# A six-layer decoder kernel on one core: ternary values fetched two banks at a time, and three small moves between engines

## The reference

```python
x = _layernorm(x + attention_int4(x))         # 32 heads, inputs and weights quantised
x = _layernorm(x + cross_attention(x, ctx))
x = _layernorm(x + expert_feedforward(x))
x = _layernorm(x + attention(x))              # 64 heads
x = _layernorm(x + long_convolution(ctx, ctx, x))
x = _layernorm(x + ternary_feedforward(x))
```

```python
def bitlinear158(x, w, b):                    # w is ternary after weight_quant
    return act_quant(rms_norm(x)) @ weight_quant(w).T + b
h = gelu(silu(bitlinear158(x, w1, b1)))       # 512 -> 2048
h = layer_norm(h, ln_g, ln_b)
x = _layernorm(x + bitlinear158(h, w2, b2))   # 2048 -> 512
```

## Time and profile before

| | us |
|---|---|
| median of three runs | 1980.08 |
| lowest, highest | 1978.74, 1982.89 |
| profiled execution, its own time | 1984.86 |
| its span, first to last instruction | 1983.1 |

### The profile page before, as it was taken

How to read it: one execution, slowest core, us unless ns; L and a number is a source line. 1 busy time by engine, 2 the same in 40 slices (tenths; PEclk the granted TensorE clock), 3 DMA queues, 4 the chain that set the end, 5 groups by cost and what they waited for, 6 DMA issues and landing times. The chain is left out here.

```text
span 1983.1 us, 32214 instructions
## 1 busy us (share of the span) xinstructions
PE 1737.2 (88%) x11756; PEld 1345.4 (68%) x11774; DVE 1398.1 (71%) x2871; ACT 1034.5 (52%) x1936; POOL 571.6 (29%) x563
## 2 busy tenths in 40 slices
PE   4489999777868999999999997999998799967876
PEld 2255665423558999999999996888886577734443
DVE  8478888587955666665665665465665699849997
ACT  3436666623414444444444444565565254469994
POOL 6133332144110001000000002223333497944321
PEclk9669999956988999999999998999998899979998
DMA  6498898051611222212222232323225265100001
GB/s 169 42 98 98 93 98 92 28 182 28 209 58 56 57 67 67 78 57 78 65 70 78 62 115 94 112 97 128 75 86 149 81 174 133 45 0 11 22 22 32
DMA packets 148480, 163.87 MB, mean 83 GB/s; under 512 B 46240, under 2 KB 100384, under 8 KB 146528
## 3 DMA queue, kind: packets, MB, share of 16 engines
q1 hardware_dynamic: 143076, 151.85, 33.8%
q10 hardware_dynamic: 5248, 9.96, 1.4%
HBM read 116.86 MB, written 19.48 MB: 69 GB/s over the span
## 5 line engine op out<-in xcount | busy, mean ns | idle before, releaser
L1661 ACT ACTIVATE f_gate<-f_gu 128x256 f32<-128x256 f32 x264 | 98.8, 383 | 270.0 <-PE f_gu L1525 190.3
L1802 DVE TENSOR_TENSOR f_hid<-f_gate,f_gu 128x256 f32<-128x256 f32 x264 | 108.2, 420 | 157.4 <-ACT f_gate L1661 153.6
L570 DVE TENSOR_REDUCE a_rowmax<-a_ring 128x2 f32<-128x512 f32 x256 | 164.9, 687 | 51.3 <-PE a_ring L652 48.9
L2826 PE MATMUL g_p<-e_kv,e_toep 128*128 128x288 f32 x640 | 164.9, 415 | 6.0 <-DVE e_planes L2885 4.2
L523 ACT ACTIVATE a_prob<-a_sT 128x1024 f32<-128x1024 f32 x128 | 130.6, 1026 | 47.7 <-PE a_sT L641 47.7
L2826 PEld LDWEIGHTS g_p<-e_kv,e_toep 128*128 128x128 f32 x640 | 122.2, 195 | 38.7 <-issue 6.6
L1538 PE MATMUL f_gu<-f_lowh,f_bg 128*128 128x256 f32 x704 | 141.5, 283 | 5.2 <-POOL f_lowl L1443 5.0
L1525 PE MATMUL f_gu<-f_xhi,f_wg 128*128 128x256 f32 x704 | 131.3, 284 | 0.0
L1525 PE MATMUL f_gu<-f_xhi,f_wu 128*128 128x256 f32 x704 | 130.4, 283 | 0.0
L1807 DVE TENSOR_TENSOR f_hl<-f_hid,f_hh 128x768 fp32r<-128x768 f32 (+2 forms) x90 | 84.5, 939 | 55.9 <-ACT f_hh L1709 54.8
L1538 PEld LDWEIGHTS f_gu<-f_lowh,f_bg 128*128 128x128 f32 x704 | 115.9, 191 | 9.8 <-POOL f_lowl L1443 5.2
(11 more groups left out here) (436 smaller groups left out, 4848.7 us busy)
## 6 DMA issues: line engine op xcount, KB each, us to landing
f_entry<-in_WdT SPq DMA_DIRECT2D x89, 256.0 KB, 2.8
d_staging<-in_w SPq DMA_DIRECT2D x16, 1024.0 KB, 5.7
a_qs<-a_hi SPq DMA_DIRECT2D x64, 128.0 KB, 7.4
a_ks<-a_hi SPq DMA_DIRECT2D x64, 128.0 KB, 6.1
e_toep<-lags SPq DMA_DIRECT2D x16, 512.0 KB, 3.9
f_entry<-in_Bg SPq DMA_DIRECT2D x89, 64.0 KB, 1.9
f_entry<-in_Bu SPq DMA_DIRECT2D x89, 64.0 KB, 2.0
cf<-in_xT SPq DMA_DIRECT2D x4, 1024.0 KB, 7.8
```

The lines of the kernel that those rows point to most:

```text
L570: dve.tensor_reduce(rowmax[:, s % 2, :, e * SLOTS + j], ring[n % RING][:, :].rearrange("p (q t) -> p q t", t=T), AX.X, ALU.max, negate=Tru ...
L1661: act.activation(gate[:, i % 2, :], gu[n % 3][:, 0, :], ACT.Silu).then_inc(s_["gate_ready"], 1)
L1802: dve.tensor_tensor(hid[:, j, :], gate[:, i % 2, :], gu[n % 3][:, 1, :], ALU.mult).then_inc(s_["hid_ready"], 1)
L2826: last = pe.matmul(py[n % RING][:, 0:YS], toep[:, u, h % 2, (t - j) * P:(t - j + 1) * P], kv[:, h % 2, j, :, :].rearrange("p b c -> p (b c ...
```

## The change

In the attention output, GpSimd keeps the bias of the first three batches (`OTHERS = 3`) and the root steps; VectorE subtracts the bias of the other five and does the residual sum of all tiles, in an instruction that also gives the row's sum, and from it the negative mean. ScalarE takes the sum of squares about the mean. Of the four token loads ahead one stays where it was, and the next stage's SP issues the other three first. In the ternary layer `pq2` is one PSUM tile of two banks, so that the 16 turns of a tile go in two groups of eight and ScalarE fetches 1024 values in one instruction, the first before the squares of s-4 and the second where the four were. GpSimd's add of the bias to tile t waits for L3198 of tile t+2, the one of the same step (for the last tiles, tile 15).

```diff
-                for b in range(3):
+                for b in range(OTHERS):
                     take_bias(b)
-                for i in range(B + 1):
-                    if i < B:
-                        n = i * TB
-                        pool.wait_ge(got_x[i], 16)
-                        pool.wait_ge(s_["y_ready"], n + 1)
-                        pool.tensor_tensor(row_of(rows, n), r[:, n % RR, :], row_of(rows, n), ALU.add
-                                           ).then_inc(s_["sum_even"], 1)
-                    if i + 3 < B:
...
-                            pool.tensor_scalar(stats[:, n, 8:9], stats[:, n, 6:7], stats[:, n, 9:10], -1.0, ALU.mult, ALU.mult
-                                               ).then_inc(s_["root_ready"], 1)
+                for n in range(NT):
+                    pool.wait_ge(s_["square_ready"], n + 1)
+                    pool.tensor_scalar(stats[:, n, 3:4], stats[:, n, 2:3], 1.0 / D, EPS, ALU.mult, ALU.add
+                                       ).then_inc(s_["eps_added"], 1)
+                    pool.wait_ge(s_["eps_added"], n + 1)
+                    pool.tensor_tensor(stats[:, n, 4:5], stats[:, n, 3:4], keep["neghalf"][:, :], ALU.pow
+                                       ).then_inc(s_["root_steps"], 1)
+                    pool.wait_ge(s_["root_steps"], n + 1)
+                    pool.tensor_tensor(stats[:, n, 5:6], stats[:, n, 1:2], stats[:, n, 4:5], ALU.mult
+                                       ).then_inc(s_["root_ready"], 1)
 
...
                 def scale(b):
-                    dve.wait_ge(s_["sub_ready"], b + 1)
+                    if b < OTHERS:
+                        dve.wait_ge(s_["sub_ready"], b + 1)
+                    else:
+                        ch.step(dve.tensor_tensor(flat[:, :, chunks(b), :], flat[:, :, chunks(b), :], wide_of(cbias, b),
+                                                  ALU.subtract))
                     dve.tensor_tensor(flat[:, :, chunks(b), :], flat[:, :, chunks(b), :], wide_of(inv, b), ALU.mult
...
                     for q in range(TB):
                         n = i * TB + q
-                        if 0 <= n < NT:
-                            dve.wait_ge(s_["acc_done"], n + 1)
-                            if n >= RR:
-                                dve.wait_ge(s_["sum_odd" if q else "sum_even"], (n - RR) // TB + 1)
-                            dve.scalar_tensor_tensor(r[:, n % RR, :], acc[n % RING][:, :], unit_tok[:, n:n + 1], wsrow[:, :],
-                                                     ALU.mult, ALU.mult).then_inc(s_["y_ready"], 1)
-                    if i < B:
-                        n = i * TB + 1
-                        dve.wait_ge(got_x[i], 16)
+                        dve.wait_ge(s_["acc_done"], n + 1)
+                        if n >= RR:
+                            dve.wait_ge(s_["summed"], n - RR + 1)
+                        dve.scalar_tensor_tensor(r[:, n % RR, :], acc[n % RING][:, :], unit_tok[:, n:n + 1], wsrow[:, :],
+                                                 ALU.mult, ALU.mult).then_inc(s_["y_ready"], 1)
+                    dve.wait_ge(got_x[i], 16)
+                    for q in range(TB):
+                        n = i * TB + q
                         dve.wait_ge(s_["y_ready"], n + 1)
-                        dve.tensor_tensor(row_of(rows, n), r[:, n % RR, :], row_of(rows, n), ALU.add
-                                          ).then_inc(s_["sum_odd"], 1)
+                        dve.tensor_tensor_reduce(row_of(rows, n), r[:, n % RR, :], row_of(rows, n), 1.0, 0.0, ALU.add, ALU.add,
+                                                 stats[:, n, 0:1]).then_inc(s_["summed"], 1)
+                        dve.wait_ge(s_["summed"], n + 1)
+                        dve.tensor_scalar(stats[:, n, 1:2], stats[:, n, 0:1], -1.0 / D, None, ALU.mult).then_inc(s_["mean_ready"], 1)
                     if i + 2 < B:
                         quantise(i + 2)
-                    for q in range(TB):
-                        n = (i - 1) * TB + q
-                        if 0 <= n < NT:
-                            dve.wait_ge(s_["sum_odd" if q else "sum_even"], n // TB + 1)
-                            tl.step(dve.bn_stats(stats[:, n, 0:6], row_of(rows, n)))
-                            dve.bn_aggr(stats[:, n, 6:8], stats[:, n, 0:6]).then_inc(s_["var_ready"], 1)
 
...
                     for q in range(TB):
+                        n = (i - 1) * TB + q
+                        if 0 <= n < NT:
+                            act.wait_ge(s_["mean_ready"], n + 1)
+                            if n >= TB:
+                                act.wait_ge(s_["square_ready"], n - 1)
+                            act.activation(junk[:, q, :], row_of(rows, n), ACT.Square, bias=stats[:, n, 1:2],
+                                           accum_out=stats[:, n, 2:3]).then_inc(s_["square_ready"], 1)
+                    for q in range(TB):
                         n = (i - 2) * TB + q
                         if 0 <= n < NT:
                             act.wait_ge(s_["root_ready"], n + 1)
-                            act.activation(row_of(rows, n), row_of(rows, n), ACT.Identity, bias=stats[:, n, 8:9],
-                                           scale=stats[:, n, 9:10])
+                            act.activation(row_of(rows, n), row_of(rows, n), ACT.Identity, bias=stats[:, n, 5:6],
+                                           scale=stats[:, n, 4:5])
 
...
                 sp.wait_ge(stored, 16 * B * TB)
-                for n in range(4):
-                    loads.tokens(sp, io, n)
+                loads.tokens(sp, io, 0)
...
+                for n in range(1, 4):
+                    loads.tokens(sp, io, n)
                 sp.dma_start(brow[:, :], io["b1"].broadcast_to([4, INNER])).then_inc(s_["b1_in"], 16)
...
-        pq2 = [mk.ps(f"g_pq2{n}", [P, 512]) for n in range(2)]
+        pq2 = mk.ps("g_pq2", [P, IT // 2 * P])
...
                     t = tile_at(s, 1)
                     if t is not None:
-                        if t >= 1:
-                            pool.wait_ge(s_["q1_ready"], t)
+                        pool.wait_ge(s_["q1_ready"], min(t + 2, NT - 1))
...
+                def second(t, half):
+                    act.wait_ge(s_["q2_turned"], t * 2 + half + 1)
+                    act.activation(q2f[:, t % 2, half * (IT // 2):(half + 1) * (IT // 2), :],
+                                   pq2[:, :].rearrange("p (j t) -> p j t", t=P), ACT.Identity, bias=minus[:, :]
+                                   ).then_inc(s_["q2f_ready"], 1)
 
...
                         act.wait_ge(s_["shifted"], t + 1)
                         act.activation(junk[:, 1, :], hc[:, t % 4, :], ACT.Square, accum_out=row2[:, t, 0:1]).then_inc(s_["ssq2"], 1)
+                    t = tile_at(s, 6)
+                    if t is not None:
+                        if t >= 2:
+                            act.wait_ge(s_["out_done"], t - 1)
...
                     t = tile_at(s, 6)
                     if t is not None:
-                        if t >= 2:
-                            act.wait_ge(s_["out_done"], t - 1)
-                        for n in range(KT):
-                            act.wait_ge(s_["q2_turned"], t * KT + n + 1)
-                            act.activation(q2f[:, t % 2, n * 4:(n + 1) * 4, :], pq2[n % 2][:, :].rearrange("p (j t) -> p j t", t=P),
-                                           ACT.Identity, bias=minus[:, :]).then_inc(s_["q2f_ready"], 1)
+                        second(t, 1)
...
+                def turn_second(t, half):
+                    if half == 0:
                         pe.wait_ge(s_["q2_ready"], t + 1)
-                    for n in range(first, last):
-                        if t * KT + n >= 2:
-                            pe.wait_ge(s_["q2f_ready"], t * KT + n - 1)
-                        for i in range(4):
-                            j = n * 4 + i
-                            block = pe.transpose(pq2[n % 2][:, i * P:(i + 1) * P], hc[:, t % 4, j * P:(j + 1) * P],
-                                                 keep["ident"][:, :])
-                        block.then_inc(s_["q2_turned"], 1)
+                    if t * 2 + half:
+                        pe.wait_ge(s_["q2f_ready"], t * 2 + half)
+                    for i in range(IT // 2):
+                        j = half * (IT // 2) + i
+                        block = pe.transpose(pq2[:, i * P:(i + 1) * P], hc[:, t % 4, j * P:(j + 1) * P], keep["ident"][:, :])
+                    block.then_inc(s_["q2_turned"], 1)
 
```

More of the change, by code:

```diff
@@ L766, in attention0_finish @@
     RING, RR = 4, 8
+    OTHERS = 3
     SPAN = KT * NC
@@ L806, in attention0_finish @@
         r = mk.sb("a2_r", [P, RR, D])
-        stats = mk.sb("a2_stats", [P, NT, 10])
+        stats = mk.sb("a2_stats", [P, NT, 6])
+        junk = mk.sb("a2_junk", [P, 2, D], BF16)
         acc = [mk.ps(f"a2_acc{i}", [P, 512]) for i in range(RING)]
@@ L811, in attention0_finish @@
```

(31 more changed lines are left out.)

13 lines of the change are left out of this document (1 added, 12 removed).

## The result

The changed kernel takes 1972.82 us (median of five runs, 1967.27 to 1974.29), the kernel before in the same session 1980.08 (five runs, 1978.74 to 1985.86). The ratio of the two is 0.9941 with a 95% interval of 0.9923 to 0.9958: 11.7 us faster, between 8.3 and 15.2. The forecast was 14.1 faster and a time of 1966.0, range 1961.5 to 1971.5: the direction and, within the interval, the size of the gain agree; the median stands 1.3 us above the range. The agreement of the totals is in part luck: by stage the forecast was 0.8 too small, 1.7 too small and 3.4 too large. The profiled executions differ by 11.9 us: 1984.86 and 1972.95, spans 1983.1 and 1971.2.

A forecast was written before the change was run, and what follows sets the result against it. The edited stages were read separately: VectorE bounds the attention output, VectorE and ScalarE are both busy 19.6 of 20 us in the ternary stage. Gains 9.5 + 1.9 + 2.7 = 14.1 us from the 1980.1 median gave 1966.0, range 1961.5 to 1971.5.

The forecast's parts named there:

- Part 1: Attention output: VectorE's batch falls from 8.79 to 6.6 us, the stage ends 9.5 us earlier, range 7 to 10.6.
- VectorE sets it: Attention output: VectorE reaches batch 7 at 453.8, TensorE alone would at 452.7, so VectorE sets the end.
- The rival of the dear add: Attention output: running-sum adds take 1.5 us each, the batch 8.1, the gain there about 3 us, total 1972.5; chance 0.10.
- Part 2: Before the fifth stage: three token loads of 0.63 us move behind the barrier, 1.9 us gained, bounds 0.5 to 1.9.
- if TensorE waits for it, the products after it wait for VectorE anyway: Fifth stage's start: tile 0's tokens, now with 2.2 us instead of 4.1, may come late without delaying the products.
- Part 3: Ternary stage: fewer VectorE collisions and wider ScalarE fetches, less a slower end, give 2.7 us, range -1 to 6.
- The steady steps 6 to 16: Ternary stage: steps gain 0.24 or 0.6 us in turn, 0.41 on average, one nothing; 3.5 us in all.
- GpSimd comes first again: Ternary stage: the 1.02 us collision moves to L3205, the period stays 12.26, 1 us is lost, total 1969.7; chance 0.12.
- One pair of fetches there loses its waits, 1.0 gained: Ternary steps 17 to 19: VectorE sets them with 4.4 to 5 us in hand; 1.0 us gained.
- The end, 2.0 lost: Ternary stage's end: first turn to products takes 4.45 us instead of 3.45, twice, so 2.0 us lost.
- the last product groups at full clock are worth 2: Ternary stage's end: a gain of 2 us if TensorE's last products run at full clock, named only with the range.
- The rival of the clock: Ternary steps: TensorE's granted clock falls, each such step is 6 us longer, three make the kernel slower, 1984; chance 0.03.

The follow-up runs named there:

- bias_on_gpsimd: Changed kernel with the bias of all eight attention-output batches on GpSimd instead of three; ratio 0.9983 to the kernel before, stage 81.61 us.
- part1_alone: Kernel before with only the attention output's part of the change; ratio 0.9943, 11.3 us faster.
- part3_alone: Kernel before with only the ternary part, wide fetch and GpSimd's later bias; ratio 0.9995, stretch 203.13 us.
- no_two_banks: Changed kernel with the four fetches from two alternating banks put back, later bias kept; ratio 0.9931 to the kernel before, stretch 202.28 us.
- early_bias: Changed kernel with GpSimd's add released where it was before, wide fetch kept; ratio 0.9943 to the kernel before, stretch 203.09 us.
- roots_swapped: Changed kernel with GpSimd's root for the output statistics ahead of that for the hidden statistics; ratio 0.9957 to the kernel before, stretch 206.26 us.
- tail_four: Changed kernel with the last two tiles turned and fetched in four one-bank pieces; ratio 0.9930 to the kernel before, stretch 200.20 us.
- parts_1_and_2: Kernel before with the attention output's and the token loads' changes, ternary stage as before; ratio 0.9921, 15.7 us faster, stretch 201.90 us.
- tail_four_warm: tail_four plus one filler of sixteen identity turns on TensorE in step 19; ratio 0.9941 to the kernel before, stretch 202.64 us.

## Why the prediction was right, and where it was not

**Part 1, right: 9.5 forecast, 10.3 measured.** Batch 6.43 against 6.6, the add with its readout and mean 0.80 from one to the next against 0.82. The step "VectorE sets it" was the one a little off: at 6.43 us a batch against TensorE's 5.94, VectorE's head start lasts until tile 14, so TensorE sets all but 0.2 us of the end. bias_on_gpsimd shows that less work on VectorE would not have helped further, at the granted clock of 0.50 that TensorE has there. The rival of the dear add fell.

**Part 2, right: 1.9 forecast, 1.8 to 1.9 measured at the start of the stage.** The barrier came 1.9 earlier, and "if TensorE waits for it, the products after it wait for VectorE anyway" is what happened: VectorE's second operand step ends at 1541.85 + 0.28 = 1542.13 and the products begin at 1542.37, behind the turns without a gap: the two are late together, within 0.2 us. The whole stretch shortened by 3.0 to 3.6, and the rest is TensorE's clock, which the forecast left out: 1.0 in the first group and 0.6 in the middle of the stage. It may not belong to the change. With the loads as before, the first group took 7.17, 7.24 and 6.62 in three kernels (before, part1_alone, part3_alone); with one load ahead, 6.16 to 6.62 in ten; with none, 7.20 in one. The group in the middle is fast in part3_alone as in the ten. The order goes with the clock in most profiles, but part3_alone has 1.2 us of this gain without it. What makes the clock rise sooner is open.

**Part 3, wrong: 2.7 forecast, -0.7 measured (-0.9 alone).** By terms:
- The steady steps 6 to 16, 3.5 forecast: 2.8 measured, at the thirteenth shift. It was 3.46 at the eleventh shift, where step 14 ends, but step 15 lost 0.7 of it. The size is near, but the gain came from other steps than forecast, so that the nearness is luck. The prediction had ten steps at 0.41, which would be 4.1, and nothing in the step with the squares of four tiles. Measured, that step gave the most, 1.15 (17.65 to 16.50), the next 1.0, and the four after it 0.29 each (11.98, 12.05, 11.98 and 11.87 us). By the single edits, the later bias alone gives 2.27 at the eleventh shift (no_two_banks; ScalarE then holds the steps at 12.15) and the wide fetch alone 1.42 (early_bias), nearly all of it in the step with the four squares (16.30); in the other steps VectorE holds it at 12.26. The rival "GpSimd comes first again" fell: L3207 keeps 2.35 in all steps but one.
- "GpSimd's add took 2.56 ... ending 1.1 after it": it takes 3.31. That did no harm, the root behind it is short.
- "One pair of fetches there loses its waits, 1.0 gained" in steps 17 to 19: a loss of 0.85 instead, after the 0.7 of step 15. This is the step of the prediction that failed. It said that VectorE sets these steps and has time in hand, and didn't ask what VectorE waits for in them. Two tiles' biases still collide (L3207 once at 3.38, L3192 once at 1.49 in step 15), and VectorE waits for GpSimd's root of the output statistics where that meets the shift. That the meeting matters is shown: in early_bias steps 17 to 19 have no such wait and are 0.9 us shorter, and in roots_swapped the place of this root costs 3.4. What brings it is shown as far as the edit: with the later bias the wait is there in seven steps or more under either fetch (changed kernel, no_two_banks), without it in one (kernel before, early_bias). How the later bias moves the root beside the shift was not followed.
- The end, 2.0 lost: the last tile lost 1.15, near the 1.0 forecast for each of the two. Tile 14 lost nothing: the changed kernel is 1.93 ahead at the last shift and 2.17 at tile 14's eviction.
- TensorE's clock in the last group, 1.7 lost: left out of the sum and named there only as "the last product groups at full clock are worth 2", in the gain's direction. The rival of the clock was looked for in the full steps, where it is 1.00 from 1840 to 1908; the gaps that the serial fetches open are at the end. tail_four, which takes the serial fetches out of the last two tiles and nothing else, shows both that they are its cause and what they cost.

A wide fetch is 1.01 us from start to start, and one of 512 values 0.57 (1.26 for two, the last one's 0.69 counted whole). Two narrow ones then cost 0.13 more than a wide one. The Trainium skill, page "VectorE: DVE Perf Modes", section on the TRN2 errata, gives ScalarE 172 cycles at 1.2 GHz on top of the elements for an instruction from PSUM, an estimated 0.14 us, and the trace agrees. A tile saved 0.6 all the same (2.59 to 2.0), since the old row also held 0.3 of waits for the turns.

```profile
1925.37 1.11 ACT L3060 ACTIVATE g_q2f<-g_pq,g_minus 128x1024 bf16<-128x1024 f32 x1 [1.77 <-PE g_pq L3118]
1926.38 1.99 ACT L3089 ACTIVATE g_junk<-g_ha,g_hs 128x2048 bf16<-128x2048 f32 x1
```

The trace agrees with the Trainium skill, page "SBUF — State Buffer", section "Who interferes with whom", by which the one of two such instructions that comes first keeps the other out for its whole length: a GpSimd root step of 0.19 us takes 2.35 beside the shift of 2.35, a VectorE step of 0.29 takes 1.87 beside a bias. The prediction used it for wide instructions only; here the short ones that others wait for decided.

## What to carry to other kernels

Read the end of a pipeline as a stage of its own: a fetch widened over two banks takes the overlap of turn and fetch away, which full steps hide and the last tile pays, together with TensorE's clock in the gaps. Keep the wide form for the steps and the narrow one for the last tiles (tail_four, a stretch of 200.2 us against 202.2 and 202.9; its total, 0.9930, can't be told from the 0.9921 of parts_1_and_2, which leaves the ternary stage alone). And when an instruction of GpSimd is moved away from a collision, look at the short instructions next to it and at who waits for them.

## What the runs showed of the hardware that was not expected

- A small VectorE instruction waits out a wide one of GpSimd in full: 0.29 us became 1.87, the length of one bias.
- The add with a running sum takes 0.68 us with both inputs in SBUF, with 0.08 for the readout, the same as from PSUM.
- The same sixteen matmuls took 3.63, 5.31 or 6.03 us. The gap right before them doesn't decide it: it was 0.78 before the 3.63 (tail_four), 1.21 before the 5.31 and 2.34 before the 6.03, but also 2.12 before a group that took 3.40. Keeping TensorE busy ahead of one group (tail_four_warm) moved the slow one to the next, behind an idle time of 3.68 us instead of 1.28.
- Twenty matmuls at the start of the fifth stage took 6.16 to 6.62 us with one load ahead, 6.62 to 7.24 with four, and 7.20 with none.
